# A vision transformer with routed experts on one core: attention scores kept in their PSUM bank, the next scores made later in a slot, queries in two buffers

## The reference

```python
h = embed(x)                                     # patches @ W.T + b, class token, positions
h = h + attn0(layernorm(h))                      # 16 heads of 16, relative bias, causal
h = h + shared_and_routed_experts(layernorm(h))  # 7 experts, top 2
h = h + attn1(layernorm(h))                      # 16 heads of 16, causal, no bias
h = h + gated_ffn(layernorm(h))

def attn(x):
    q, k, v = heads(x @ Wq), heads(x @ Wk), heads(x @ Wv)
    s = einsum('bhtd,bhsd->bhts', q, k) / sqrt(16) + bias    # bias is -inf above the diagonal
    return merge(einsum('bhts,bhsd->bhtd', softmax(s), v)) @ Wo + bo
```

## Time and profile before

| | us |
|---|---|
| Runs of the kernel before | 1228.11 median (1226.44 to 1228.93) |
| The profiled execution's own time | 1229.97 |
| Its span, first to last instruction | 1228.1 |
| TensorE busy | 1070.6 (87%) |
| VectorE busy | 628.7 (51%) |
| ScalarE busy | 616.5 (50%) |
| GpSimd busy | 391.6 (32%) |
| Mean granted TensorE clock | 0.931 of full |

### The profile page before, as it was taken

How to read it: one execution, slowest core, us unless ns; L and a number is a source line. 1 busy time by engine, 2 the same in 40 slices (tenths; PEclk the granted TensorE clock), 3 DMA queues, 4 the chain that set the end, 5 groups by cost and what they waited for, 6 DMA issues and landing times.

```text
span 1228.1 us, 28332 instructions
## 1 busy us (share of the span) xinstructions
PE 1070.6 (87%) x10404; PEld 904.6 (74%) x10405; DVE 628.7 (51%) x1174; ACT 616.5 (50%) x1035; POOL 391.6 (32%) x271
## 2 busy tenths in 40 slices
PE   5989799888979986999999999980579898969998
PEld 5877677766667665888888888870467777769998
DVE  3236577733323324666666666640156767724443
ACT  3446466644434432555555555540275556535554
POOL 2145345335333433122211122220444545341110
PEclk9989899989889987999999999995678999889999
DMA  6550000062111113010111110104100000000000
GB/s 224 193 219 3 4 2 3 3 281 52 21 20 20 20 20 94 31 34 32 32 34 34 34 33 31 34 26 107 51 25 30 32 1 2 3 1 21 20 10 31
DMA packets 30818, 57.45 MB, mean 47 GB/s; under 512 B 12892, under 2 KB 22314, under 8 KB 29588
## 3 DMA queue, kind: packets, MB, share of 16 engines
q1 hardware_dynamic: 16184, 44.06, 10.4%
q0 software_dynamic: 13328, 10.66, 3.2%
q10 hardware_dynamic: 1228, 1.60, 0.4%
HBM read 41.51 MB, written 14.67 MB: 46 GB/s over the span
## 4 chain that ended last, share of the span: by engine, by line
PE 56%; issue 11%; DVE 10%; POOL 10%; ACT 9%; DMA 3%; SPq 0%; DVEq 0%; ACTq 0%; POOLq 0%
PE ps L1189 19%; PE ps L1194 11%; PE ps L1196 9%; PE ps L1195 9%; POOL routed_in L454 7%; DVE Sb L846 5%; PE ps L1567 2%; DVE mx L841 2%; ACT RTs L618 2%; ACT vts L598 1%; DMA x_in<-in_xT_dram 1%; ACT RTs L616 1%; DMA yg<-routed_out 1%; POOL xn L388 1%; PE ps L1300 1%
## 5 line engine op out<-in xcount | busy, mean ns | idle before, releaser
L478 POOL DMA_INDIRECT routed_out<-yt,tile_to x43 | 65.4, 1521 | 289.5 <-DVE yt L1124 289.5
L1102 DVE TENSOR_TENSOR tile_w<-arena,tile_w 128x1408 fp32r<-128x1408 f32 x86 | 139.3, 1621 | 35.7 <-ACT tile_w L776 35.7
L1189 PE MATMUL ps<-arena,shared 128*128 x516 | 130.9, 395 | 1.0 <-ACT shared L772 1.0
L1194 PE MATMUL ps<-tile_w,xTs 128*128 128x352 f32 x344 | 120.1, 349 | 2.4 <-DVE xTs L1107 2.4
L776 ACT ACTIVATE tile_w<-arena 128x1408 fp32r x86 | 118.2, 1375 | 6.6 <-issue 6.6
L941 DVE TENSOR_TENSOR Hd<-Sg,ps 128x296 f32<-128x296 f32 x96 | 44.4, 462 | 146.4 <-ACT Sg L717 140.3
L765 ACT ACTIVATE shared<-ps 128x352 f32<-128x352 f32 x86 | 39.9, 463 | 145.8 <-PE ps L1196 141.4
L1196 PE MATMUL ps<-tile_w,xTs 128*128 128x352 f32 x344 | 112.0, 326 | 0.0
L1195 PE MATMUL ps<-tile_w,xTs 128*128 128x352 f32 x344 | 111.9, 325 | 0.0
L1189 PEld LDWEIGHTS ps<-arena,shared 128*128 128x128 f32 x516 | 90.8, 189 | 28.0 <-issue 15.6
L1189 PE MATMUL ps<-xn,shared 128*128 128x296 f32 x352 | 109.2, 457 | 0.0
(11 more groups left out here) (195 smaller groups left out, 2648.0 us busy)
## 6 DMA issues: line engine op xcount, KB each, us to landing
arena<-in_ew_dram SPq DMA_DIRECT2D x7, 2176.0 KB
x_in<-in_xT_dram SPq DMA_DIRECT2D x7, 888.0 KB, 4.9
xt<-routed_in SPq DMA_DIRECT2D x43, 129.0 KB, 2.0
yg<-routed_out SPq DMA_DIRECT2D x8, 592.0 KB
out_dram<-h SPq DMA_DIRECT2D x8, 296.0 KB, 2.7
routed_in<-zero_x SPq DMA_DIRECT2D x13, 129.0 KB, 10.5
gu_i<-in_gu_dram SPq DMA_DIRECT2D x1, 1536.0 KB, 21.5
shared<-in_gu_dram SPq DMA_DIRECT2D x1, 1408.0 KB, 7.5
```

The source lines that it names most:

```text
L478: pool.indirect_dma_start(ys, bass.IndirectOffsetOnAxis(tile_to[b][:, 0:1], 0), yt[b][:], None).then_inc(s_yt, 16)
L1102: dve.tensor_tensor(tile_w[half][1], gate_up_of(w, half), tile_w[half][0].bitcast(F32), ALU.subtract).then_inc(s.wl, 1)
L1189: return pe.matmul(out_, lhsT, rhs, start=start, stop=stop)
L1194: pe.matmul(out_, w[1], x[0], start=start, stop=False)
```

## The change

VectorE's `scaled` writes its result back into banks 0 and 1, where it read it. `greatest` reads the banks. `centred` reads the banks and writes `Sb`, and now it is the one that waits for the exponential that read this `Sb` before (`a.ex`). The banks are thus in use until the centring is over, so `scores` on TensorE waits for `a.sc` (the centring before) and not for `a.sb`. Its call moves in every slot from behind `probs_t` to just ahead of `outputs`. Since projections of the next group's queries now come ahead of the last scores of this group, the queries get two buffers, `QT0` and `QT1`; the second lies in memory that the embedding stage has used.

```diff
-        QT = carve("QT", DK, N)
+        QT = [carve("QT0", DK, N)]
...
         xa.append(halves("xa1", DK, N))
+        QT.append(carve("QT1", DK, N))
...
-                        act.activation((KT, QT)[k // DK][:, k % DK], src, ACT.Identity,
+                        act.activation((KT, QT[b])[k // DK][:, k % DK], src, ACT.Identity,
...
+                in_bank = ps[:, 0:2, 0:DK * HW].rearrange("p r (h k) -> p r h k", k=T)
+
                 def scaled(n, p):
                     b = p % 2
                     dve.wait_ge(a.S_mm, FREE + n + 1)
-                    dve.wait_ge(a.ex, n + 1)
                     halves_of = lambda t: t.rearrange("p (r h) k -> p r (h k)", r=2)
-                    dve.scalar_tensor_tensor(out=halves_of(Sb[b]), in0=ps[:, 0:2, 0:DK * HW], scalar=HD ** -0.5,
+                    dve.scalar_tensor_tensor(out=ps[:, 0:2, 0:DK * HW], in0=ps[:, 0:2, 0:DK * HW], scalar=HD ** -0.5,
                                              in1=halves_of(bias[l][:]), op0=ALU.mult, op1=ALU.add).then_inc(a.sb, 1)
 
                 def greatest(n, p):
                     b = p % 2
                     dve.wait_ge(a.sb, FREE + n + 1)
-                    dve.tensor_reduce(mx[b][:], Sb[b], AX_X, ALU.max).then_inc(a.mx, 1)
+                    dve.tensor_reduce(mx[b][:].rearrange("p (r h) -> p r h", r=2), in_bank, AX_X, ALU.max).then_inc(a.mx, 1)
 
                 def centred(n, p):
                     b = p % 2
                     dve.wait_ge(a.mx, FREE + n + 1)
-                    dve.tensor_tensor(Sb[b], Sb[b], mx[b][:].unsqueeze(2).to_broadcast([P, HEADS, T]),
-                                      ALU.subtract).then_inc(a.sc, 1)
+                    dve.wait_ge(a.ex, n + 1)
+                    most = mx[b][:].rearrange("p (r h) -> p r h", r=2).unsqueeze(3).to_broadcast([P, 2, HP, T])
+                    dve.tensor_tensor(Sb[b].rearrange("p (r h) k -> p r h k", r=2), in_bank, most, ALU.subtract).then_inc(a.sc, 1)
...
-                def scores(n, g, p):
+                def scores(n, g, gb, p):
                     pe.wait_ge(a.km, FREE + n + 1)
-                    pe.wait_ge(a.sb, FREE + n)
+                    pe.wait_ge(a.sc, FREE + n)
...
                     if not X.first:
                         at("out1p", out_proj, g - 1, 1)
                     if not X.last:
-                        scores(n + 5, g + 1, 1)
                         at("proj5", project, g + 1, 1 - b, 5)
+                    if not X.last:
+                        scores(n + 5, g + 1, 1 - b, 1)
                     at("O3", outputs, n + 3, 3)
```

More of the change, by code:

```diff
@@ L584, in attention, with project @@
                     act.sem_inc(buf_free, FREE)
-                def project(g, k, bk):
+                def project(g, b, k, bk):
                     act.wait_ge(a.proj_mm, 6 * g + k + 1)
@@ L650, in attention @@
                 for k in range(4):
-                    project(0, k, (2, 3, 7, 6)[k])
+                    project(0, 0, k, (2, 3, 7, 6)[k])
                 deviation(a, 1, 2)
-                project(0, 4, 6)
-                project(0, 5, 3)
+                project(0, 0, 4, 6)
+                project(0, 0, 5, 3)
                 upper_x(a, 1, 1, xa[1])
@@ L668, in step @@
                     if not X.last:
-                        project(g + 1, 0, X.bank("proj0"))
-                        project(g + 1, 1, X.bank("proj1"))
+                        project(g + 1, 1 - b, 0, X.bank("proj0"))
+                        project(g + 1, 1 - b, 1, X.bank("proj1"))
                     shares(n, 0, X.bank("O0"))
@@ L679, in step @@
                     if not X.last:
-                        project(g + 1, 2, X.bank("proj2"))
-                        project(g + 1, 3, X.bank("proj3"))
+                        project(g + 1, 1 - b, 2, X.bank("proj2"))
+                        project(g + 1, 1 - b, 3, X.bank("proj3"))
                     shares(n + 1, 1, X.bank("O1"))
@@ L689, in step @@
                         deviation(*norm_ahead(l, g, X), X.bank("var"))
-                        project(g + 1, 4, X.bank("proj4"))
+                        project(g + 1, 1 - b, 4, X.bank("proj4"))
                     shares(n + 2, 2, X.bank("O2"))
@@ L701, in step @@
                         exps(n + 4, 0)
-                        project(g + 1, 5, X.bank("proj5"))
+                        project(g + 1, 1 - b, 5, X.bank("proj5"))
                 over_body(act, l, step)
@@ L1291, in scores @@
                                 ins = mm(ps[i * PITCH:i * PITCH + T, r, c * HW:(c + 1) * HW],
-                                         QT[rows, c, q0:q0 + T], Km[p % 2][rows, c, :, i * T:(i + 1) * T])
+                                         QT[gb][rows, c, q0:q0 + T], Km[p % 2][rows, c, :, i * T:(i + 1) * T])
                     ins.then_inc(a.S_mm, 1)
@@ L1376, in attention @@
                 project(0, 0, 5, 3)
-                scores(0, 0, 0)
-                scores(1, 0, 1)
+                scores(0, 0, 0, 0)
+                scores(1, 0, 0, 1)
                 def step(g, b, X):
@@ L1391, in step @@
                         at("comb1", lambda bk: routed_out(g + 2, b, 1, bk))
-                    scores(n + 2, g, 2)
                     at("V0", values, n, g, 0)
@@ L1397, in step @@
                         at("proj1", project, g + 1, 1 - b, 1)
+                    scores(n + 2, g, b, 2)
                     at("O0", outputs, n, 0)
@@ L1404, in step @@
                         at("mean", mean, *norm_ahead(l, g, X))
-                    scores(n + 3, g, 3)
                     at("V2", values, n + 2, g, 2)
@@ L1409, in step @@
                         at("proj3", project, g + 1, 1 - b, 3)
+                    scores(n + 3, g, b, 3)
                     at("O1", outputs, n + 1, 1)
@@ L1414, in step @@
                         at("out0p", out_proj, g - 1, 0)
-                    if not X.last:
-                        scores(n + 4, g + 1, 0)
                     at("V3", values, n + 3, g, 3)
@@ L1420, in step @@
                         at("proj4", project, g + 1, 1 - b, 4)
+                    if not X.last:
+                        scores(n + 4, g + 1, 1 - b, 0)
                     at("O2", outputs, n + 2, 2)
```

## The result

| | before | changed |
|---|---|---|
| Median of four runs each, side by side | 1228.52 us (1226.44 to 1231.0) | 1210.89 us (1209.79 to 1211.65) |
| The profiled execution's own time; its span | 1229.97; 1228.1 | 1209.79; 1207.9 |
| Mean granted TensorE clock | 0.931 | 0.933 |

What follows compares the result with a forecast made beforehand. TensorE bounds the two attention stages, waiting at group boundaries for exponentials held by the centring. From the profiled 1229.97 us, less 2.9 (layer 0) and 12.0 (layer 1), 1215.1; the median lies 1.86 lower: 1213 us, range 1204 to 1221.

Steps and rivals of the forecast that it cites:

- The centring at 0.76, always: VectorE's centring, reading PSUM like the scaling, takes 0.76 us always; 1.23 less where TensorE waited for it at 209.74.
- PSUM accesses for nothing: VectorE's scaling, maximum and centring pay nothing for using PSUM; upper bound another 0.76 us for an instruction.
- An ordinary boundary gains 0.9, period near 19.75: Steady group boundary: 1.0 us gained before the next transposes, less 0.1 in slot 0; the group's period was 20.65.
- Layer 0, 2.9: Layer 0's attention stage gains 2.9 us: 3.6 + 0.6 - 0.65 + 0.5 - 1.2 over boundaries, prologue and last group.
- the first has no output projection and no gain: The first of layer 0's seven group boundaries has no output projection and was given no gain.
- the loop's stalls: Layer 0 boundary where TensorE stands 3.86 us for its own instructions: old wait hidden, slot 3's new one not, -0.65.
- Layer 1, 12.0: Layer 1's attention stage gains 12.0 us: 3.3 + 3.6 + 1.55 + 1.2 - 0.7 + 3.0, the last for the clock.
- of the 1.46: Layer 1: TensorE was busy 1.46 us longer at clock 0.93; 1.0 of it regained in each of three merging groups, 3.0.
- this wait goes too: Layer 1's merging groups: TensorE's wait before slot 2 goes, four of them at 0.8 to 0.9 us, 3.3.
- rival 1: The clock is not given back at the same places: 3.0 us less gain, 1216 us; chance 0.2.
- Rival 2: Slot 3's wait is hidden too (6.0 us) and the clock stays up over merging groups (1.4): 1206 us; chance 0.2.
- Rival 3: PSUM bank is the bound: scores wait in the slots, loss from x about 0.4 a chain, near 1290 us; chance 0.06.

Runs made afterwards that it cites:

- both reorderings: The changed kernel with the maximum ahead of the normalisation in every slot and, in slot 3, the centring ahead of the residual: 1192.79 us, ratio 0.9704.

## Why the prediction was right, and where its sizes were off

It forecast 1213 us (1204 to 1221) and faster; the median is 1210.89. By its steps:

- **The centring at 0.76, always**: right (760 to 776 ns), and for the reason given, which the run with GpSimd's instruction cut short shows from the other side.
- **PSUM accesses for nothing**: nearly. Two of the three lines became longer, by 23 and 6 ns, some 0.03 a chain. The Trainium skill ("Perfetto Trace Analysis", section "Optimizing Scalar/DVE Operations") gives about 60 ns of access overhead for SBUF and 125 for PSUM, which makes an estimate of 65 ns for each; the trace does not agree.
- **An ordinary boundary gains 0.9, period near 19.75**: right in sum (19.66, 19.82, 19.87), by terms that partly offset one another. Slot 3 had 4.50 and measured 4.56 (its scores 3.21 from the start, predicted 3.15). Slot 0 had 0.1 more than 4.55 and measured 4.74 and 4.89. In slots 1 and 2 the prediction had no gain, and each is 0.12 shorter (5.18). In slot 0 I had looked at the wrong resource: not the scores wait but the transposes of V ahead of them, for a bank that the normalisation of slot 3 must have read first (L1303 waits for L865 seven times, 2.4 us in all).
- **Layer 0, 2.9**: measured 4.6. The terms that failed are "the first has no output projection and no gain" and the full clock taken for granted beside it. Groups 0 and 1 took 41.89 together and now 39.98, at a clock of 0.97 and 0.94 where it was 0.87 and 1.00: 1.9 gained, against the 0.9 in the sum. The prologue gave 0.8 (0.5 in the sum), the last group took 1.4 (1.2 in the sum). The rest is in the two groups around the loop's stalls. The stalls cost 6.73 now (4.49 and 2.24) and 6.28 before: 0.45, where I had 0.65. But TensorE's busy time in these two groups fell by 1.4 (42.2 to 40.8), so that they gained 1.0 together, where the sum had 0.25. The sum for layer 0 had no term for busy time.
- **Layer 1, 12.0**: measured 14.3, from terms that were off in both directions. The four merging groups gained 13.9 (9.9 in the sum). Here the attribution failed, not only the size: TensorE's idle time in them fell by 4.6, where the sum had 6.9 for waits, and its busy time by 9.3, where the sum had 3.0 for the clock. That the layer's total came within 2.3 us is luck in part. In the group of the earlier trace rows idle time went from 2.68 to 1.91, by 0.8, where the sum had 1.7 for two waits: one wait of 0.73 before the scores and one of 0.46 before the next transposes came in, and the one for the merged rows grew from 0.30 to 0.71. TensorE's busy time fell by 1.93, where I had taken 1.0 "of the 1.46". The row at a granted clock of 1.00 that I measured by, busy for 20.11, was itself above the 19.64 that the same work needs. And "this wait goes too", put down to the centring's operand, goes by the order of the scores alone. The first group gave 0.2 and not 1.2: its wait of 1.88 before the transposes came back as one of 1.90 before the scores. The last took 2.4 and not about 1.2: 1.0 of it is idle time, and 1.4 is busy time at a granted clock of 0.75 (0.82 before). In layer 0 the last group lost 1.4 by idle time nearly alone; the two waits before scores that no projection covers are these.

```profile
229.68 0.72 PE L1192 MATMUL ps<-Km,QT 64*37 64x148 f32 x16 [1.37 <-issue]
...
233.91 0.72 PE L1192 MATMUL ps<-Km,QT 64*37 64x148 f32 x16 [1.67 <-issue]
```

- **The rivals.** The clock was given back, so rival 1 fell. Rival 2 was half right: the clock stood at 1.00 over the merging groups, while slot 3's wait stayed. Its price was too low: with both reorderings that wait is gone, and the time is 18 us less, where it had 7. But they also took from the last groups' waits (1.37 and 1.67 became 0.73 and 0.87 in layer 0), so the 18 are not slot 3's alone. Rival 3, the bank as the bound, was the real danger, and its turning point was set too far off: it had x = 0.4. With nothing added the ratio is 0.9855 and with 0.7 it is 1.0209, which puts it at about 0.3 if the line between is straight. Slots 1 and 3 became longer nearly as written (by 0.28 and 0.81, where it had 0.35 and 0.7 for x = 0.7); slot 0 had no wait before its scores in that group and 0.42 in the next, where it had 0.8. The price left out the clock, which doubled it.

What stays open is why slots 1 and 2 are 0.12 shorter each. The pieces are the same and stand in another order; no run took them apart. Open too is how much of the clock each wait costs: against the kernel before, TensorE's idle and busy time moved the same way in every run, in no fixed ratio.

## What to carry to other kernels

When an instruction on VectorE has lengths of 0.76 and 2.8 for one shape, look at what GpSimd runs beside it and which operands are in SBUF. One operand in PSUM freed it here for 0.03 us; but first look at whether an earlier place in the engine's own queue is free, since moving the maximum ahead of a wait gave 2.0% where this change gave 1.5%, and both with the residual moved too gave 3.0%. A buffer that is held for longer must be asked for later: the same PSUM chain was 7.6% slower with the scores at their old place. And a wait on TensorE is to be priced with its clock: with the doubled maximum 23.5 us more of idle time over both stages went with 23.3 us more of busy time.

## What was not expected of the hardware

- VectorE and GpSimd, both on SBUF: beside `lower_x` the one that began first keeps its length, and the other is held. VectorE behind: 1.99 instead of 0.76. GpSimd behind: 2.00 instead of 1.44 (`lower_x`), 1.72 instead of 1.19 (the mask).
- Who began first does not decide everywhere. Behind the merging the mask began 0.8 to 1.0 after the centring that was already waiting, kept its short length (1.17 to 1.20), and the centring was held through both. It is so in all five such meetings before (2.64 to 2.80) and in all five of that kernel with the maximum moved (2.71 to 2.81). Behind `lower_x` the waiting centring came ahead of the mask. What makes the difference no run shows.
- Writing 592 fp32 elements of a row back into the two PSUM banks they were read from took 783 ns, 23 more than writing them to SBUF.
- The granted clock over a stretch (the share of 2.4 GHz; below 1.00 a part ran at 1.2) fell with modest waits: 0.94 at 0.78 of idle time in 20.70 (97.17), 1.00 at 0.73 in 19.66 (186.85), 0.93 at 2.37 in 23.08 and, over three slots, 0.78 at 5.28 in 22.94. The first pair shows that idle time of the group alone does not say which clock is granted.
